# Self-attention's output projection as three f16 products from a z held in two f16 parts, with the next batch normalised one step earlier

## The chip, the cores and the metric

One core of one Trainium2 chip runs the whole program. The metric is the device time of one execution in microseconds (us). Engines are named as in the profile: PE is TensorE's matmul, PEld its weight load, DVE is VectorE, ACT is ScalarE, POOL is GpSimd, SP is SyncE.

## The reference

A decoder block over 32 batches of 128 tokens of width 128, in f32: self attention (16 heads of 64, causal), cross attention (16 heads of 8, with 128 context rows), and a mixture of 8 experts. The change touches self attention alone, and in it the last product and the normalisation of the input:

```
x = _layernorm(resid_stream, ln_w, ln_b)
...
pattern = jax.nn.softmax(scores, axis=-1)
z = jnp.einsum('bhqk,bkhe->bqhe', pattern, v)
attn_out = jnp.einsum('bqhe,hed->bqd', z, W_o) + b_o
```

## The kernel before

The program has three stages one after the other: self attention over all 32 batches, cross attention over all batches, and the experts. The last two batches of self attention are interleaved with the first steps of cross attention (`run_joined`).

Self attention is written out by hand as a pipeline over batches, and every engine runs the same function `self_attention(b, parity, valid, steps)` for b = -2 up to 32. Each batch has four steps g = 0 to 3. In one pass over b the engines work on three batches: the input of batch b+2 is normalised and transposed, the projections q, k, v of batch b+1 are made, the scores and softmax of batch b are made, and z and the output of batch b-1 are made. `valid(k)` says whether batch b+k exists. Each engine works through its own list in the order written; semaphores alone order the engines, and there are no queues or planners between them.

What the change touches, in one batch:

- Step 2, PE: z of batch b-1 as 32 entries of small f32 products into two PSUM banks, ps0 and ps1 (semaphore `sa_z_in_bank`). ACT copies each bank into the SBUF tile `zT` (L554, `sa_z_taken`).
- Step 2, DVE: the sums of unit 2 (L667, L670), then `xn`, the normalised input of batch b+2 (L720), which waits for `rstd` from POOL (`sa_rstd`, L395).
- Step 3, PE: transposes `xn` into ps7 (L979), transposes one more unit of probabilities (L1022), waits for `sa_z_taken` and for `sa_xT_taken`, and then multiplies `zT` by `wo`: eight f32 products of 128x128 that add up in another part of ps7 (L1033, shown by the profile as L971, the helper `mm`).
- Step 3, DVE: takes the transposed input out of ps7 as `xT` (L677, `sa_xT_taken`), sums unit 3, and adds the output to the residual `x_all` (L726) after `sa_output`.
- The next pass begins on PE with the scores of units 0 and 1, for which DVE's `nmax` (L660) waits.

An f32 product is one matmul in the code and two entries in the profile's counts. The projections q, k, v (`w1_hi`, `w1_lo`, `xT_hi`, `xT_lo`) are already made in three f16 products: high by high, high by low, low by high.

Of the kernel before, what the change touches and what calls it, by code (L numbers as in the profile page):

```python
# [23 lines left out]
P = 128  # L24
# [24 lines left out]
NORM_SCALE = 256.0  # L49
W_SCALE = 256.0  # L50
H_SCALE = 16.0
MASKED = -3.0e38


# [44 lines left out]
def build(nc, x, ctx, W_q, W_k, W_v, W_o, b_q, b_k, b_v, b_o, ln_w, ln_b, w_qkv, w_proj, b_proj,  # L99
          gate_w, gate_proj_w, up_proj_w, down_proj_w, out):  # L100
    es = ExitStack()
    with es:
# [27 lines left out]
        w1_hi = sb("w1_hi", [P, 3, H, E1], F16)  # L130
        w1_lo = sb("w1_lo", [P, 3, H, E1], F16)
        wo = sb("wo", [P, PAIRS, D])
        bq = sb("bq", [P, PAIRS])
        bk = sb("bk", [P, PAIRS])
        bv = sb("bv", [P, PAIRS])
# [22 lines left out]
        probs = sb("probs", [P, 4, 512])  # L158
        probsT = sb("probsT", [P, 4, 512])
        zT = sb("zT", [P, PAIRS, P])  # L160
        nmax = sb("nmax", [P, 8, 4])
        rsum = sb("rsum", [P, 8, 4])
        rinv = sb("rinv", [P, 8, 4])
# [82 lines left out]
        sa_scores = sem("sa_scores"); sa_max = sem("sa_max"); sa_exp = sem("sa_exp")  # L246
        sa_sums = sem("sa_sums"); sa_inverse_sums = sem("sa_inverse_sums")
        sa_probs = sem("sa_probs"); sa_pT_in_bank = sem("sa_pT_in_bank"); sa_pT_taken = sem("sa_pT_taken")
        sa_z_in_bank = sem("sa_z_in_bank"); sa_z_taken = sem("sa_z_taken"); sa_output = sem("sa_output")
        sa_residual = sem("sa_residual")  # L250

        ca_stats = sem("ca_stats"); ca_mean_var = sem("ca_mean_var"); ca_var_eps = sem("ca_var_eps")
# [258 lines left out]
        def _(act):  # L511
# [8 lines left out]
            for i, w in enumerate((wq, wk, wv)):  # L520
                act.wait_ge(qkv_loaded[i], 16)
                nc.scalar.activation(w1_hi[:, i, :, :], w[:, :, :], ACT.Copy, scale=W_SCALE).then_inc(w1_high_ready, 1)

            def self_attention(b, parity, valid, steps):
                def copy_transposed(g):
                    off, u, _ = back(b, parity, g, 2, G1)
                    if valid(off):
                        act.wait_ge(sa_pT_in_bank, G1 * (b + off) + u + 1)
                        nc.scalar.copy(probsT[:, u, :], ps[6][:, :]).then_inc(sa_pT_taken, 1)  # L529

                def exponentials(u):
                    if valid(0):
                        act.wait_ge(sa_max, G1 * b + u + 1)
                        for i in range(HPG):
                            last = nc.scalar.activation(probs[:, u, i * P:(i + 1) * P],  # L535
                                                        ps[u][:, i * P:(i + 1) * P], ACT.Exp,
                                                        bias=nmax[:, u, i:i + 1])
                        last.then_inc(sa_exp, 1)

                for g in steps:  # L540
                    if g == 0:
                        copy_transposed(0)
                        exponentials(0)
                        exponentials(1)
                    if g == 1:
                        copy_transposed(1)
                        exponentials(2)
                    if g == 2 and valid(-1):
                        n = b - 1
                        if valid(-2):  # L550
                            act.wait_ge(sa_output, n)
                        for half in range(HALVES):
                            act.wait_ge(sa_z_in_bank, HALVES * n + half + 1)
                            nc.scalar.copy(zT[:, 4 * half:4 * half + 4, :], ps[half][:, :]).then_inc(sa_z_taken, 1)  # L554
                    if g == 2:
                        copy_transposed(2)
                        exponentials(3)
                    if g == 3:
                        copy_transposed(3)
                    if g == 3 and valid(1):  # L560
                        n, np_ = b + 1, (parity + 1) % 2
                        for half in range(2):
                            act.wait_ge(sa_projected, 6 * n + 5 + half)
                            nc.scalar.activation(v1[:, np_, 512 * half:512 * half + 512], ps[4 + half][:, :], ACT.Copy,
                                                 scale=1.0 / (X1_SCALE * W_SCALE)).then_inc(sa_v_taken, 1)
# [85 lines left out]
        def _(dve):  # L651
# [4 lines left out]
            def self_attention(b, parity, valid, steps):  # L656
# [15 lines left out]
                for g in steps:  # L672
                    if g == 3 and valid(2):
                        dve.wait_ge(sa_xT_in_bank, b + 3)
                        if valid(1):
                            dve.wait_ge(sa_x_low, b + 2)
                        nc.vector.tensor_scalar(xT[:, :], ps[7][:, 0:P], lnwb[:, 0:1], lnwb[:, 1:2],  # L677
                                                ALU.mult, ALU.add).then_inc(sa_xT_taken, 1)

                    if g == 0:  # L680
                        maximum(0)
                        maximum(1)
                    if g == 1:
                        sums(0, 0)
                        maximum(2)
                        sums(0, 1)
                        maximum(3)
                    if g >= 2:
                        sums(0, g)

                    if valid(1) and g < 2:
                        n, np_ = b + 1, (parity + 1) % 2
                        for half in range(2):
                            dve.wait_ge(sa_projected, 6 * n + 2 * g + half + 1)
                            tiles = ps[4 + half][:, :].rearrange("p (t q) -> p t q", t=4)
                            own = slice(4 * half, 4 * half + 4)
                            if g == 0:
                                last = nc.vector.scalar_tensor_tensor(  # L698
                                    out=qT[:, np_, own, :], in0=tiles,
                                    scalar=E1 ** -0.5 / (X1_SCALE * W_SCALE), in1=bcast(bq[:, own], P),  # L700
                                    op0=ALU.mult, op1=ALU.add)
                            else:
                                last = nc.vector.scalar_tensor_tensor(
                                    out=kT[:, np_, own, :], in0=tiles, scalar=1.0 / (X1_SCALE * W_SCALE),
                                    in1=bcast(bk[:, own], P), op0=ALU.mult, op1=ALU.add)
                            last.then_inc(sa_qk_taken, 1)

                    if valid(2):
                        n = b + 2
                        if g == 0:  # L710
                            if valid(-2) and not valid(-3):
                                dve.wait_ge(x_rest_loaded, 16)
                            dve.sem_inc(alone)
                            nc.vector.bn_stats(bst[:, 0, :], x_all[:, n, :]).then_inc(sa_stats, 1)
                            dve.wait_ge(sa_stats, n + 1)
                            dve.sem_inc(alone)
                            nc.vector.bn_aggr(mv[:, 0, :], bst[:, 0, :]).then_inc(sa_mean_var, 1)
                        if g == 2:
                            dve.wait_ge(sa_rstd, n + 1)
                            nc.vector.tensor_scalar(xn[:, :], x_all[:, n, :], mv[:, 0, 0:1], rstd[:, 0:1],  # L720
                                                    ALU.subtract, ALU.mult).then_inc(sa_norm, 1)
                    if g == 3 and valid(-1):
                        n = b - 1
                        dve.wait_ge(sa_output, n + 1)
                        dve.wait_ge(sa_bias_added, n + 1)
                        nc.vector.tensor_tensor(x_all[:, n, :], ps[7][:, P:2 * P], x_all[:, n, :],  # L726
                                                ALU.add).then_inc(sa_residual, 1)

            def prepare():

# [12 lines left out]
            def prepare_cross():  # L743
# [8 lines left out]
                for dst, i, f in ((wqR, 0, E2 ** -0.5), (wkR, 1, 1.0)):  # L752
                    nc.vector.memset(dst[:, :, :, 3, :], 0.0).then_inc(quad_weights_ready, 1)
                    for t in range(4):
                        heads = wqkvT[:, i, 32 * t:32 * t + 32].rearrange("p (l e) -> p l e", e=E2)
                        nc.vector.tensor_scalar(dst[:, t, :, 0:3, :], heads.unsqueeze(2).to_broadcast([P, 4, 3, E2]),
                                                f, None, ALU.mult).then_inc(quad_weights_ready, 1)

                dve.wait_ge(bv_wo_summed, 1)
                dve.wait_ge(row_biases_loaded, 32)  # L760
# [208 lines left out]
        def _(pe):  # L969
# [3 lines left out]
            def self_attention(b, parity, valid, steps):  # L973
                for g in steps:
# [50 lines left out]
                    if g == 3 and valid(-1):  # L1025
                        n = b - 1
                        pe.wait_ge(sa_z_taken, HALVES * n + HALVES)
                        if valid(2):
                            pe.wait_ge(sa_xT_taken, b + 3)
                        if not valid(1):  # L1030
                            pe.wait_ge(ca_xT_taken, 1 if valid(0) else 2)
                        for i in range(PAIRS):
                            last = mm(ps[7][:, P:2 * P], zT[:, i, :], wo[:, i, :], i == 0, i == PAIRS - 1)  # L1033
                        last.then_inc(sa_output, 1)
                    if valid(1) and g < 3:

# [286 lines left out]
```

## Time and profile before

| what | value |
|---|---|
| runs | 1156.07, 1158.15, 1158.4 us; median 1158.15 us |
| the profiled execution's own time | 1158.08 us |
| its span, first to last instruction | 1156.2 us |
| busy: PE, PEld | 1074.3 us (93%), 800.0 us (69%) |
| busy: DVE, ACT, POOL | 830.5 us (72%), 674.7 us (58%), 457.6 us (40%) |
| mean granted TensorE clock | 0.981 of full speed |

The steady part of self attention lies between about 47 and 435 us of the span, and one batch takes 13.41 us there. Times in a row are from the span's start. A group of several instructions is printed as one row: its start, the time from there to the end of the last one, and after "x" their count. The bracket at a row's end is the idle time before it and what ended that.

### The profile page before, as it was taken

Reading aid. Unit: us, or ns where it says so; the run is one execution under the profiler, and the core shown is the slowest. Engines: PE = TensorE matmul, PEld = TensorE weight load, DVE = VectorE, ACT = ScalarE, POOL = GpSimd, SP = SyncE. Lnnn points to the kernel's source line nnn. Section 1 sums busy time; section 2 is a strip of 40 time slices with the busy share of each in tenths; the row PEclk is TensorE's granted clock in tenths of the full one; section 3 lists DMA queues with packets and bytes.
Section 4 is the critical chain, followed back from the end, with each engine's and each line's share of the span. In section 5 each row is a group of like instructions: output and inputs, shape, how many; then the busy total and the mean of one; then the engine's idle time right before and its main releaser. Section 6 shows DMA issues by size and latency. Waiting matters only on the chain.

```text
span 1156.2 us, 30982 instructions
## 1 busy us (share of the span) xinstructions
PE 1074.3 (93%) x12235; PEld 800.0 (69%) x12235; DVE 830.5 (72%) x1921; ACT 674.7 (58%) x1510; POOL 457.6 (40%) x799
## 2 busy tenths in 40 slices
PE   5999999999999998989999999999966999999997
PEld 4788888888888886667767677677643666565664
DVE  4776667776667774677777777777737788888887
ACT  2666666666656665555555565565534755555554
POOL 3444444444444444244344354453322522222222
PEclk9999999999999999899999999999976999999999
DMA  7000000000000000000000000002100000000000
GB/s 169 2 2 2 2 2 2 1 2 2 2 1 2 2 1 10 11 11 15 11 15 11 11 16 11 12 16 68 55 1 0 2 10 11 11 10 11 10 11 10
DMA packets 20658, 16.01 MB, mean 14 GB/s; under 512 B 7042, under 2 KB 18596, under 8 KB 20516
## 3 DMA queue, kind: packets, MB, share of 16 engines
q1 hardware_dynamic: 20176, 13.90, 4.6%
q8 instruction: 98, 1.61, 0.6%
q10 hardware_dynamic: 340, 0.14, 0.1%
q14 instruction: 44, 0.36, 0.1%
HBM read 11.94 MB, written 2.10 MB: 12 GB/s over the span
## 4 chain that ended last, share of the span: by engine, by line
PE 64%; issue 18%; DVE 8%; POOL 7%; ACT 2%; DMA 1%; SPq 0%; DVEq 0%; POOLq 0%
PE ps L971 56%; POOL h_lo L500 5%; PE ps L1022 5%; ACT q_shifted L572 2%; PE ps L1183 1%; DVE xT L677 1%; DMA wv<-in_L_attn_W_v 1%; DVE bst L852 1%; DVE x_all L848 1%; POOL probs L385 1%; PE ps L1213 1%; DVE padded L789 1%; DVE mv L855 1%; PE ps L1201 0%; PE ps L979 0%
## 5 line engine op out<-in xcount | busy, mean ns | idle before, releaser
L807 DVE TENSOR_REDUCE nmax<-ps 128x2 f32<-128x512 f32 x256 | 164.7, 686 | 15.4 <-PE ps L971 15.4
L597 ACT ACTIVATE probsT<-ps 128x512 f32<-128x512 f32 x256 | 139.7, 603 | 41.9 <-PE ps L971 41.0
L500 POOL TENSOR_TENSOR h_lo<-wk,h_hi 128x512 f16<-128x512 f32 x64 | 73.9, 1155 | 185.7 <-ACT h_hi L641 182.8
L535 ACT ACTIVATE probs<-ps,nmax 128x128 f32<-128x128 f32 x512 | 143.1, 384 | 6.9 <-DVE nmax L660 6.9
L529 ACT COPY probsT<-ps 128x512 f32<-128x512 f32 x128 | 75.2, 587 | 116.3 <-PE ps L1022 116.3
L385 POOL TENSOR_TENSOR probs<-probs,rinv 128x512 f32<-128x512 f32 x128 | 133.0, 1040 | 15.9 <-DVE rinv L670 15.9
L971 PE MATMUL ps<-probsT,va 128*32 128x128 f32 x2048 | 137.8, 277 | 0.0
L633 ACT ACTIVATE wq<-ps 128x512 f32<-128x512 f32 x128 | 76.6, 598 | 73.7 <-PE ps L971 73.6
L971 PEld LDWEIGHTS ps<-probsT,va 128*32 128x32 f32 x2048 | 103.0, 110 | 17.0 <-issue 6.7
L660 DVE TENSOR_REDUCE nmax<-ps 128x4 f32<-128x512 f32 x128 | 83.5, 673 | 38.9 <-PE ps L971 38.9
L955 DVE TENSOR_TENSOR h_lo<-wk,h_hi 128x512 f16<-128x512 f32 x64 | 71.8, 1122 | 43.8 <-ACT h_hi L641 43.8
L971 PE MATMUL ps<-xnT_hi,w_hi 128*128 128x512 f16 x256 | 99.7, 389 | 2.7 <-DVE wk L950 2.7
L641 ACT CAST h_hi<-wk 128x512 f16<-128x512 f32 x128 | 77.9, 618 | 40.6 <-DVE wk L950 40.5
L971 PE MATMUL ps<-xnT_lo,w_hi 128*128 128x512 f16 x256 | 99.2, 387 | 0.0
L971 PE MATMUL ps<-xnT_hi,w_lo 128*128 128x512 f16 x256 | 99.0, 387 | 0.0
L971 PE MATMUL ps<-xT_hi,w_hi 128*128 128x128 f16 x512 | 91.2, 222 | 6.2 <-DVE raw_gu L698 4.2
L971 PE MATMUL ps<-xT_lo,w_hi 128*128 128x128 f16 x512 | 91.3, 222 | 0.0
L971 PE MATMUL ps<-xT_hi,w_lo 128*128 128x128 f16 x512 | 91.3, 222 | 0.0
L971 PE MATMUL ps<-w_hi,h_hi 128*128 128x128 f16 x512 | 88.9, 219 | 2.6 <-DVE h_lo L955 2.6
L971 PE MATMUL ps<-w_hi,h_lo 128*128 128x128 f16 x512 | 89.0, 219 | 0.0
L971 PE MATMUL ps<-w_lo,h_hi 128*128 128x128 f16 x512 | 88.9, 219 | 0.0
L667 DVE TENSOR_REDUCE rsum<-probs 128x4 f32<-128x512 f32 x128 | 85.9, 671 | 3.7 <-ACT probs L535 3.7
(204 smaller groups left out, 2552.3 us busy)
## 6 DMA issues: line engine op xcount, KB each, us to landing
ctx_row<-in_ctx SPq DMA_DIRECT2D x32, 128.0 KB, 2.0
out_x<-x_all SPq DMA_DIRECT2D x8, 256.0 KB, 2.3
kT<-in_L_ffn_down_proj_w SPq DMA_DIRECT2D x1, 1024.0 KB, 10.8
wq<-in_L_attn_W_q SPq DMA_DIRECT2D x1, 512.0 KB, 5.0
wk<-in_L_attn_W_k SPq DMA_DIRECT2D x1, 512.0 KB, 8.8
wv<-in_L_attn_W_v SPq DMA_DIRECT2D x1, 512.0 KB, 10.4
wo<-in_L_attn_W_o SPq DMA_DIRECT2D x2, 256.0 KB, 6.7
x_all<-in_x SPq DMA_DIRECT2D x1, 256.0 KB, 3.0
```

Of the source, the lines that this page charges most:

```text
L385: nc.gpsimd.tensor_tensor(pr, pr, bcast(rinv[:, u, :], P), ALU.mult).then_inc(sa_probs, 1)
L500: nc.gpsimd.tensor_tensor(h_lo[:, e % 2, 0, :], hT[:, 0, :], h_hi[:, e % 2, 0, :], ALU.subtract).then_inc(hidden_low_first, 1)
L529: nc.scalar.copy(probsT[:, u, :], ps[6][:, :]).then_inc(sa_pT_taken, 1)
L535: last = nc.scalar.activation(probs[:, u, i * P:(i + 1) * P], ps[u][:, i * P:(i + 1) * P], ACT.Exp, bias=nmax[:, u, i:i + 1])
L597: last = nc.scalar.activation(probsT[:, 2 * (t % 2) + a, :], ps[2 + a][:, :], ACT.Exp)
L633: nc.scalar.activation(silu[:, i, :], ps[i][:, :], ACT.Silu, scale=1.0 / (NORM_SCALE * W_SCALE)).then_inc(silu_ready, 1)
L641: nc.scalar.copy(h_hi[:, e % 2, i, :], hT[:, i, :]).then_inc(hidden_high, 1)
L660: nc.vector.reduce_max(nmax[:, u, :], ps[u][:, :].rearrange("p (h k) -> p h k", h=HPG), AX_X, negate=True).then_inc(sa_max, 1)
L667: nc.vector.reduce_sum(rsum[:, u, :], probs[:, u, :].rearrange("p (h k) -> p h k", h=HPG), AX_X).then_inc(sa_sums, 1)
L807: last = nc.vector.reduce_max(nmax2[:, b % 2, t:t + 2, l + a], ps[a][:, :].rearrange("p (t k) -> p t k", t=2), AX_X, negate=True)
L955: nc.vector.tensor_tensor(h_lo[:, e % 2, 1, :], hT[:, 1, :], h_hi[:, e % 2, 1, :], ALU.subtract).then_inc(hidden_low_second, 1)
L971: return nc.tensor.matmul(o, l, r, start=start, stop=stop, **kw)
```

## The change

z is no longer copied as f32. ACT writes four times z as f16 (`zT_hi`), DVE writes what is left over of four times z as f16 (`zT_lo`), and both lie in the memory of the old tile `zT`. The weight `wo` is split once, at the start, into `wo_hi` and `wo_lo` (times 256). The output is 24 f16 products in place of eight f32 ones, and the residual addition divides by the scales. On DVE `xn` moves from step 2 to the end of step 1.

```diff
+            act.wait_ge(wo_loaded, 32)
+            nc.scalar.activation(wo_hi[:, :, :], wo[:, :, :], ACT.Copy, scale=W_SCALE).then_inc(wo_high_ready, 1)
...
                         for half in range(HALVES):
                             act.wait_ge(sa_z_in_bank, HALVES * n + half + 1)
-                            nc.scalar.copy(zT[:, 4 * half:4 * half + 4, :], ps[half][:, :]).then_inc(sa_z_taken, 1)
+                            nc.scalar.activation(zT_hi[:, 4 * half:4 * half + 4, :], ps[half][:, :], ACT.Copy,
+                                                 scale=Z_SCALE).then_inc(sa_z_high, 1)
...
                     if g >= 2:
                         sums(0, g)
+                    if g == 2 and valid(-1):
+                        for half in range(HALVES):
+                            dve.wait_ge(sa_z_high, HALVES * (b - 1) + half + 1)
+                            nc.vector.scalar_tensor_tensor(
+                                out=zT_lo[:, 4 * half:4 * half + 4, :], in0=ps[half][:, :].rearrange("p (t q) -> p t q", t=4),
+                                scalar=Z_SCALE, in1=zT_hi[:, 4 * half:4 * half + 4, :], op0=ALU.mult,
+                                op1=ALU.subtract).then_inc(sa_z_taken, 1)
...
-                        if g == 2:
+                        if g == 1:
                             dve.wait_ge(sa_rstd, n + 1)
                             nc.vector.tensor_scalar(xn[:, :], x_all[:, n, :], mv[:, 0, 0:1], rstd[:, 0:1],
                                                     ALU.subtract, ALU.mult).then_inc(sa_norm, 1)
...
-                        nc.vector.tensor_tensor(x_all[:, n, :], ps[7][:, P:2 * P], x_all[:, n, :],
-                                                ALU.add).then_inc(sa_residual, 1)
+                        nc.vector.scalar_tensor_tensor(out=x_all[:, n, :], in0=ps[7][:, P:2 * P],
+                                                       scalar=1.0 / (Z_SCALE * W_SCALE), in1=x_all[:, n, :],
+                                                       op0=ALU.mult, op1=ALU.add).then_inc(sa_residual, 1)
...
+                dve.wait_ge(wo_high_ready, 1)
+                nc.vector.scalar_tensor_tensor(out=wo_lo[:, :, :], in0=wo[:, :, :], scalar=W_SCALE, in1=wo_hi[:, :, :],
+                                               op0=ALU.mult, op1=ALU.subtract).then_inc(wo_low_ready, 1)
...
                         pe.wait_ge(sa_z_taken, HALVES * n + HALVES)
+                        if n == 0:
+                            pe.wait_ge(wo_low_ready, 1)
...
                         for i in range(PAIRS):
-                            last = mm(ps[7][:, P:2 * P], zT[:, i, :], wo[:, i, :], i == 0, i == PAIRS - 1)
+                            for k, (z, w) in enumerate(((zT_hi, wo_hi), (zT_hi, wo_lo), (zT_lo, wo_hi))):
+                                last = mm(ps[7][:, P:2 * P], z[:, i, :], w[:, i, :], i == 0 and k == 0,
+                                          i == PAIRS - 1 and k == 2)
```

On DVE, in every steady batch, the list before reads as follows from the end of step 1 (`kT`) to the residual of step 3. The names are those of the kernel, and the bracket names the semaphores waited for.

```order
L703 SCALAR_TENSOR_TENSOR kT<-ps,bk 128x512 [waits sa_projected] x2
L667 TENSOR_REDUCE rsum<-probs 128x4 [waits sa_exp]
L670 RECIPROCAL rinv<-rsum 128x4 [waits sa_sums]
L720 TENSOR_SCALAR xn<-x_all,mv,rstd 128x128 [waits sa_rstd]
L677 TENSOR_SCALAR xT<-ps,lnwb 128x128 [waits sa_x_low,sa_xT_in_bank]
```

The same place in the changed kernel, whose lines are numbered differently (L719 is the old L703, L736 the old L720, L686 the old L677):

```order
L719 SCALAR_TENSOR_TENSOR kT<-ps,bk 128x512 [waits sa_projected] x2
L736 TENSOR_SCALAR xn<-x_all,mv,rstd 128x128 [waits sa_rstd]
L676 TENSOR_REDUCE rsum<-probs 128x4 [waits sa_exp]
L679 RECIPROCAL rinv<-rsum 128x4 [waits sa_sums]
L702 SCALAR_TENSOR_TENSOR zT<-ps,zT 128x512 [waits sa_z_high] x2
L686 TENSOR_SCALAR xT<-ps,lnwb 128x128 [waits sa_x_low,sa_xT_in_bank]
```

`xn` now stands ahead of the sums of unit 2, and the two new instructions for `zT_lo` stand between those sums and `xT`. On PE, in step 3 and at the head of the next pass, the list before is:

```order
L979 MATMUL ps<-ident,xn 128x128 [waits sa_residual,sa_norm]
L1022 MATMUL ps<-ident,probs 128x128 [waits sa_pT_taken,sa_probs]
L1022 MATMUL ps<-ident,probs 128x128 x3
L971 MATMUL ps<-wo,zT 128x128 [waits sa_xT_taken,sa_z_taken]
L971 MATMUL ps<-wo,zT 128x128 x7
L971 MATMUL ps<-causal,ident_b 128x512 [waits sa_exp,sa_qk_taken]
```

In the changed kernel the eight `wo` products of that list are 24, in this pattern; `zT` is `zT_hi` in the first two of each three and `zT_lo` in the third:

```order
L1000 MATMUL ps<-ident,xn 128x128 [waits sa_residual,sa_norm]
L1043 MATMUL ps<-ident,probs 128x128 [waits sa_pT_taken,sa_probs]
L1043 MATMUL ps<-ident,probs 128x128 x3
L992 MATMUL ps<-wo_hi,zT 128x128 [waits sa_xT_taken,sa_z_taken]
L992 MATMUL ps<-wo_lo,zT 128x128
L992 MATMUL ps<-wo_hi,zT 128x128 x2
...
L992 MATMUL ps<-causal,ident_b 128x512 [waits sa_exp,sa_qk_taken]
```

Nothing else moved on PE, and the waits are the same two, but `sa_z_taken` is now signalled by DVE, not by ACT.

## Rows read from the trace of the kernel before

**Rows 1.** The page: busy time by engine, and granted clock in 40 slices.

```profile
PE 1074.3 (93%) x12235; PEld 800.0 (69%) x12235; DVE 830.5 (72%) x1921; ACT 674.7 (58%) x1510; POOL 457.6 (40%) x799
...
PEclk9999999999999999899999999999976999999999
```

**Rows 2.** One batch's window (length, busy by engine, clock), and PE's idle time until xT (us, times).

```profile
288.68:302.09 13.41, 13.25 (x157) 10.97 (x156) 9.34 (x21) 8.67 (x25) 5.91 (x9) 1.00 0.00 1
...
  DVE xT L677: 4.6, 29
```

**Rows 3.** The chain of waits in one batch: start, length, what.

```profile
302.32 0.42 DVE xT L677
...
302.88 3.55 PE ps L971 x34
```

**Rows 4.** Timeline of PE and PEld around the output product, and a first f16 product.

```profile
289.44 1.86 PEld L971 LDWEIGHTS ps<-wo,zT 128*128 128x128 f32 x16 [0.37 <-issue]
289.47 2.02 PE L971 MATMUL ps<-wo,zT 128*128 128x128 f32 x16 [0.16 <-DVE xT L677]
...
291.33 0.60 PE L971 MATMUL ps<-causal,ident_b 128*128 128x512 bf16 x2
...
292.95 0.66 PE L1022 MATMUL ps<-ident,probs 128*128 128x128 f32 x4
...
293.33 0.10 PEld L971 LDWEIGHTS ps<-xT_hi,w_hi 128*128 128x128 f16 x1
...
293.44 0.22 PE L971 MATMUL ps<-xT_hi,w_hi 128*128 128x128 f16 x1
```

**Rows 5.** Timeline of PE in the experts: the first of 24 products, and what follows them.

```profile
902.54 0.22 PE L971 MATMUL ps<-w_hi,h_hi 128*128 128x128 f16 x1
...
903.88 0.38 PE L971 MATMUL ps<-xnT_hi,w_hi 128*128 128x512 f16 x1
```

**Rows 6.** Timeline of DVE in one batch, end of step 1 to step 3.

```profile
298.86 1.28 DVE L703 SCALAR_TENSOR_TENSOR kT<-ps,bk 128x512 f32<-128x512 f32 x2
300.05 0.68 DVE L667 TENSOR_REDUCE rsum<-probs 128x4 f32<-128x512 f32 x1
300.76 0.18 DVE L670 RECIPROCAL rinv<-rsum 128x4 f32<-128x4 f32 x1
300.86 0.32 DVE L720 TENSOR_SCALAR xn<-x_all,mv,rstd 128x128 f32<-128x128 f32 x1
302.32 0.41 DVE L677 TENSOR_SCALAR xT<-ps,lnwb 128x128 f32<-128x128 f32 x1 [1.14 <-PE ps L979]
```

**Rows 7.** Timeline of ACT and POOL near it.

```profile
290.27 1.04 POOL L385 TENSOR_TENSOR probs<-probs,rinv 128x512 f32<-128x512 f32 x1
...
300.34 0.58 ACT L554 COPY zT<-ps 128x512 f32<-128x512 f32 x1 [0.23 <-PE ps L971]
```

**Rows 8.** DVE's groups by shape: busy us, mean ns, idle before.

```profile
L955 DVE TENSOR_TENSOR h_lo<-wk,h_hi 128x512 f16<-128x512 f32 x64 | 71.8, 1122 | 43.8 <-ACT h_hi L641 43.8
...
L776 DVE SCALAR_TENSOR_TENSOR q_part<-q_hi,low_q,ps 128x512 f16<-128x512 f16 x32 | 23.6, 737 | 1.4 <-ACT q_hi L585 1.4
...
L739 DVE SCALAR_TENSOR_TENSOR w_lo<-wq,w_hi 128x1024 f16<-128x1024 f32 x1 | 1.2, 1226 | 0.0
```

**Rows 9.** Timeline of DVE before the first scores.

```profile
25.72 0.17 DVE L761 TENSOR_SCALAR gateT<-ps 128x8 f32<-128x8 f32 x1 [0.26 <-PE ps L971]
...
27.36 1.29 DVE L660 TENSOR_REDUCE nmax<-ps 128x4 f32<-128x512 f32 x2 [0.87 <-PE ps L971]
```

**Rows 10.** Timeline where self attention joins cross attention (b = 31, 32).

```profile
446.39 1.21 ACT L554 COPY zT<-ps 128x512 f32<-128x512 f32 x2
...
447.00 0.72 DVE L776 SCALAR_TENSOR_TENSOR q_part<-q_hi,low_q,ps 128x512 f16<-128x512 f16 x1
...
447.77 1.16 PE L971 MATMUL ps<-xT,wkR 128*128 128x128 f32 x8 [0.61 <-DVE q_part L776]
...
456.58 2.05 PE L971 MATMUL ps<-wo,zT 128*128 128x128 f32 x16 [0.68 <-ACT zT L554]
```

More of the change, by code:

```diff
@@ L51 @@
 H_SCALE = 16.0
+Z_SCALE = 4.0
 MASKED = -3.0e38
@@ L132, in build @@
         wo = sb("wo", [P, PAIRS, D])
+        wo_hi = sb("wo_hi", [P, PAIRS, D], F16)
+        wo_lo = sb("wo_lo", [P, PAIRS, D], F16)
         bq = sb("bq", [P, PAIRS])
@@ L160, in build @@
         zT = sb("zT", [P, PAIRS, P])
+        zT_halves = zT[:, :, :].rearrange("p t q -> p (t q)").bitcast(F16).rearrange("p (a t q) -> p a t q", a=2, t=PAIRS)
+        zT_hi, zT_lo = zT_halves[:, 0, :, :], zT_halves[:, 1, :, :]
         nmax = sb("nmax", [P, 8, 4])
@@ L248, in build @@
         sa_probs = sem("sa_probs"); sa_pT_in_bank = sem("sa_pT_in_bank"); sa_pT_taken = sem("sa_pT_taken")
-        sa_z_in_bank = sem("sa_z_in_bank"); sa_z_taken = sem("sa_z_taken"); sa_output = sem("sa_output")
+        sa_z_in_bank = sem("sa_z_in_bank"); sa_z_high = sem("sa_z_high"); sa_z_taken = sem("sa_z_taken"); wo_high_ready = sem("wo_high_ready"); wo_low_ready = sem("wo_low_ready"); sa_output = sem("sa_output")
         sa_residual = sem("sa_residual")
```

## The prediction

> **What bounds the kernel now.** First the page: PE is busy 93% of the span, and the granted clock is 0.9 or more of full speed in all the slices of self attention, the first 16 [rows 1]. Then the window of one batch: 13.41 us long with PE busy 13.25, DVE 9.34, ACT 8.67, POOL 5.91, at clock 1.00, the 2.4 GHz level [rows 2]. So PE bounds the batch, and what it does not fill is small. Then the chain of waits in that batch, to see whether PE is alone: the chain leaves PE at one place only, for DVE's xT, which starts at 302.32 and lets PE go on at 302.88 with the output product [rows 3]. The reader is to see that an instruction of PE saved behind that point shortens the batch, and that an instruction of DVE added ahead of xT lengthens it once DVE's own slack is used up. PE waits for xT in 29 batches [rows 2]; those are the steady ones.
>
> **Step 1, the product itself.** After the wait the weight load of the f32 product starts at 289.44 and the next work, the causal mask, starts at 291.33: 1.89 us for the eight products [rows 4]. The f16 price is in this kernel already: 24 products of the same shape, three parts for each piece, added up in one PSUM region, run in the experts from 902.54 to 903.88, which is 1.34 us or 56 ns each [rows 5]. After a gap an f16 load starts 0.11 ahead of its product (293.33, 293.44) [rows 4]. So the new stretch is 0.11 + 1.34 = 1.45 us, and PE saves 1.89 - 1.45 = **0.44 us** a batch. The other bound: reckoned from product to product it is 291.33 - 289.47 = 1.86 against 1.34, 0.52. I take 0.44, since the wait in front exposes the first load here.
>
> **Step 2, the work added on DVE.** Two instructions of 128x512, PSUM and f16 in, f16 out, stand between the sums of unit 2 and xT. The trace has no such form. Nearest are the kT pair: same instruction, one operand in PSUM, an immediate scalar; two of them end 1.28 after their start and the next instruction starts at 300.05, 1.19 after it, so each occupies **0.60** although it is 0.68 long [rows 6]. The f16 output costs nothing there: 1024 elements out of SBUF in this very form take 1.226 us, no more than twice 0.61 [rows 8]. The form with f16 in and out and PSUM is 0.737 long, about 0.06 more, but it has a per-partition scalar where the new one has an immediate [rows 8]; by it each would occupy 0.66. I take 0.60, for the immediate.
>
> **Step 3, what covers it.** DVE has xn started at 300.86 and xT at 302.32, 1.46 apart with 1.14 idle between them, waiting for PE's transpose of xn [rows 6]. xn itself occupies 0.32 less the overlap of 0.08 that the kT pair shows, 0.24. The free stretch is 1.46 - 0.24 = 1.22 us. xn moves ahead of the sums, which shifts them by 0.24 and leaves the total as it was. The new pair needs 2 x 0.60 = 1.20. So xT can start 0.02 before PE's transpose lets it: the cover just suffices, and I put the lateness at **0**. With 0.66 each it is 1.32 - 1.22 = 0.10 late, and with 0.74 each, end to end, 0.26. Without the move of xn the transpose would have waited for the pair; with it, xn is ready at about 300.4 and PE asks for it about 302.
>
> The pair's own wait, for ACT's second half, is not felt: ACT ends it at 300.92 [rows 7], and DVE comes to the second at 300.29 + 0.71 + 0.10 + 0.60 = 301.70 (the sums 0.24 later than 300.05, the spacing of the sums and the reciprocal as in [rows 6]). Behind the pair wait xT and the sums of unit 3, nothing else. The scale and the f16 output on ACT stand in the place of a copy of the same size and I put them at nothing; their cover is the 0.78 between 300.92 and 301.70.
>
> **Step 4, does the gain survive the round?** After the output product PE goes to the scores, for which DVE has been waiting; both move up together. The first later wait that is not PE's own is for the probabilities of unit 2: POOL's multiplication starts at 290.27 and takes 1.04, so it ends at 291.31 [rows 7], while PE asks for them after the mask and the scores, at 292.95 [rows 4]. With PE 0.44 earlier 1.2 us are left. So the steady batches give 29 x 0.44 = **12.8 us**.
>
> **Step 5, the ends.** At the start ACT splits wo once and DVE once; DVE's part takes what one of the same shape takes, 1.23, and occupies 1.15 [rows 8]. DVE there has 0.26 idle before gateT and 0.87 before the first nmax, 1.13 in all [rows 9]: nothing, or 0.02. Where b = 30 there is no xT to wait for and PE saves its 0.44. Where b = 31, DVE's q_part of cross attention now stands behind the pair: ACT ends the two z halves at 446.39 + 1.21 = 447.60, the second zT_lo takes 447.64 to 448.32, q_part starts at 448.26, not at 447.00, and PE has been waiting for it [rows 10]. That costs 1.26, less the 0.44 of the product: +0.82. Where b = 32 nothing covers the last zT_lo. The f32 product starts there at 456.58, released by ACT, and ends at 458.63 [rows 10]; now zT_lo takes that start and 0.68, to 457.26, with 0.04 to PE, and then 0.11 + 23 x 0.056 + 0.22 for the 24 products gives 458.92: +0.29. The ends sum to -0.44 + 0.82 + 0.29 = +0.7.
>
> **Sum.** -12.8 + 0.7 = -12.1. The profiled execution took 1158.08 us for its span of 1156.2, and the median of the runs is 1158.15, the same within 0.1. 1158.1 - 12.1 = **1146.0 us**.
>
> **The rivals.**
>
> *A, DVE becomes the bound by a little (17%).* Speaking for it: the cover in step 3 is 0.02 us, that is, none. If the two instructions occupy their full 0.68, xT is 0.14 late; at 0.74, 0.26 late. The gain is then 0.30 to 0.18 a batch, 8.7 to 5.2 in all, and the time 1158.1 - 8.7 + 0.7 = 1150.1 to 1153.6. Against it: the kT pair overlaps. The Trainium skill, "VectorE: DVE Perf Modes", section "The DRAIN you can't avoid", says that the next operation does not start until the pipe is empty. By that rule each would occupy its whole length; here the rows after the kT pair, starting 0.09 before its end, speak against so much [rows 6].
>
> *B, slower (6%).* The new instruction runs like L955, the subtraction of an f16 part from an f32 one with f16 out: 1.122 long [rows 8], 1.04 occupied. Then xT is 2.08 - 1.22 = 0.86 late, the batch longer by 0.86 - 0.44 = 0.42, and the time 1158.1 + 12.2 + 0.7 = 1171. It decides from (1.22 + 0.44) / 2 = 0.83 occupied each. Against it: L955 reads both operands from SBUF, but so does L739, at 1.226 for twice the elements [rows 8], so that the slowness is not of the form alone; the new one reads one from PSUM, as kT does. The Trainium skill, "SBUF — State Buffer", section "Terms", says that VectorE and GpSimd hold a shared port pair exclusively and that the loser blocks.
>
> *C, the f16 products don't run at 56 ns (3%).* The loads are 0.10 long [rows 4]; if each stood in front of its product, 24 would take 2.4 us and the batch would be 0.6 longer, 1158.1 + 18 = 1176. It decides from 1.78 / 24 = 74 ns. The experts' rows speak against it [rows 5].
>
> *D, the gain is swallowed by another wait (4%).* Time 1158 to 1159, with the 0.7 of the ends. Step 4 leaves 1.2 us at the nearest.
>
> **How the numbers follow.** The forecast has 70%. Its own range is 1143 (0.52 a batch, 30 batches, +0.7) to 1149.0 (0.34 a batch: 0.10 late). To leave out no more than 2 in 10 the range takes in A: 1143 to 1153.6. B, C and D, 13%, are left out. A difference under 0.2% (2.3 us) can't be told from no change here. Faster by more: the forecast and A, and a little is taken off for what joins them, 0.88. Within it: D, 0.05. Slower: B and C, 0.07.
>
> **What the profile would show.** Right: the batch is 12.97 long; the 24 products fill about 1.4 us between xT's release and the mask; DVE's idle time before xT is gone or under 0.1; PE's transpose of xn waits for nothing. Step 2 is wrong if the pair takes over 1.3 us; step 1 if the stretch after the wait is not 1.45; step 4 if PE has a new wait elsewhere in the batch. The forecast is wrong, above all, if the pair starts late or lasts longer, because nothing is left between it and xT.

## The result, and the profile after

| | before | changed |
|---|---|---|
| median of the runs | 1158.2 us (1156.07 to 1158.4, 4 runs) | 1142.51 us (1141.44 to 1143.47, 4 runs) |
| ratio, 95% interval | | 0.9868 (0.9851 to 0.9886) |
| run again later | 1157.94 us (9 runs) | 1143.12 us (4 runs), 0.9879 (0.9865 to 0.9893) |
| profiled execution: time, span | 1158.08, 1156.2 us | 1141.44, 1139.7 us |

The change is faster by 15.7 us, where 12.1 was forecast; the median lies 0.5 us below the stated range, and the repeat 0.1 above its lower end. The way was right, the size was not. The kernel before ran again beside every later run, with medians of 1157.6 to 1157.9 us; every ratio below is to those.

The page of the changed kernel, busy time by engine and the granted clock in 40 slices, to be held against [rows 1]:

```profile
PE 1052.5 (92%) x12458; PEld 782.9 (69%) x12491; DVE 868.7 (76%) x1986; ACT 676.6 (59%) x1511; POOL 457.5 (40%) x799
...
PEclk9999999999999999999999999999977999999999
```

DVE is up by 38 us, the 64 new instructions less what overlaps, and PE is down by 22. Some 3 of these 22 are not real: this trace lacks 33 of PE's 12491 product records, and in the repeat, which has all of them, PE is at 1055.8 us. The timeline of DVE over one steady batch shows where that work went, where [rows 6] had 1.14 us of idle time:

```profile
282.69 1.29 DVE L669 TENSOR_REDUCE nmax<-ps 128x4 f32<-128x512 f32 x2 [1.24 <-PE ps L992]
...
288.48 1.28 DVE L719 SCALAR_TENSOR_TENSOR kT<-ps,bk 128x512 f32<-128x512 f32 x2
289.67 0.34 DVE L736 TENSOR_SCALAR xn<-x_all,mv,rstd 128x128 f32<-128x128 f32 x1
289.93 0.68 DVE L676 TENSOR_REDUCE rsum<-probs 128x4 f32<-128x512 f32 x1
290.64 0.18 DVE L679 RECIPROCAL rinv<-rsum 128x4 f32<-128x4 f32 x1
290.74 1.26 DVE L702 SCALAR_TENSOR_TENSOR zT<-ps,zT 128x512 f16<-128x512 f32 x2
291.94 0.41 DVE L686 TENSOR_SCALAR xT<-ps,lnwb 128x128 f32<-128x128 f32 x1
...
295.57 1.29 DVE L669 TENSOR_REDUCE nmax<-ps 128x4 f32<-128x512 f32 x2 [1.24 <-PE ps L992]
```

Two things are to be seen. The pair takes 290.74 to xT at 291.94, 1.20 us, and no idle time is printed ahead of xT any more. And the batch, from one nmax to the next, is 295.57 - 282.69 = 12.88 us. Over 27 steady batches the mean is 12.886, 0.52 shorter than the 13.407 of the kernel before.

The timeline of PE and PEld in the same batch, for [rows 4]:

```profile
291.63 0.27 PE L1000 MATMUL ps<-ident,xn 128*128 128x128 f32 x1
...
292.47 0.10 PEld L992 LDWEIGHTS ps<-wo_hi,zT 128*128 128x128 f16 x1 [0.37 <-issue]
292.50 0.22 PE L992 MATMUL ps<-wo_hi,zT 128*128 128x128 f16 x1 [0.16 <-DVE xT L686]
```

The record of the first product of the causal mask, which follows the 24, is missing in this batch. The repeat of the same kernel has it:

```profile
292.64 0.22 PE L992 MATMUL ps<-wo_hi,zT 128*128 128x128 f16 x1 [0.16 <-DVE xT L686]
...
293.98 0.59 PE L992 MATMUL ps<-causal,ident_b 128*128 128x512 bf16 x2
```

So the 24 products take 1.34 us, 56 ns each. And in the kernel before, the transpose of xn stands here:

```profile
302.01 0.27 PE L979 MATMUL ps<-ident,xn 128*128 128x128 f32 x1
```

PE's transpose of xn waits for nothing in the changed kernel either, and xT starts 0.31 behind it, as before (302.01 and 302.32). The first load stands 0.03 ahead of its product, and the product starts 0.56 behind the start of xT (291.94, 292.50). With f32 it was 302.32 and 302.88, 0.56 too [rows 3]. The f16 load costs nothing extra at this place.

The chain of waits of the changed kernel has moved, though no wait has grown (start, length, what):

```profile
290.01 0.61 DVE rsum L676
...
290.74 1.26 DVE zT L702 x2
291.99 0.37 DVE xT L686
292.37 0.14 issue
292.50 1.50 PE ps L992 x24
```

(The 1.50 reaches to the end of the last product and not to the start of the next work, which is why it is more than 1.34.) It runs through DVE from nmax to xT, since both engines arrive there within 0.05 us of each other (the run with a third instruction, below). That the chain changes its engine says that they are level, not that one of them has become slower.

### The profile page after: what moved, and what is told of

Same layout as the page of the kernel before. It is cut to its first block, busy times and chain, and to the rows that moved or that the text cites. A ratio compares the mean times of both kernels' runs of the same rounds, so it can differ in the third digit from the quotient of the medians.

```text
span 1139.7 us, 31527 instructions
## 1 busy us (share of the span) xinstructions
PE 1052.5 (92%) x12458; PEld 782.9 (69%) x12491; DVE 868.7 (76%) x1986; ACT 676.6 (59%) x1511; POOL 457.5 (40%) x799
## 3 DMA queue, kind: packets, MB, share of 16 engines
q1 hardware_dynamic: 20176, 13.90, 4.6%
## 4 chain that ended last, share of the span: by engine, by line
PE 41%; DVE 29%; issue 19%; POOL 6%; ACT 3%; DMA 1%; DVEq 0%; SPq 0%; POOLq 0%
PE ps L992 37%; DVE nmax L669 6%; POOL h_lo L505 6%; DVE rsum L676 5%; DVE zT L702 3%; DVE kT L719 3%; DVE raw_gu L714 2%; ACT q_shifted L581 2%; PE ps L1208 1%; DVE rinv L679 1%; DVE xT L686 1%; DMA wv<-in_L_attn_W_v 1%; DVE bst L873 1%; DVE x_all L869 1%; DVE bst L730 1%
## 5 line engine op out<-in xcount | busy, mean ns | idle before, releaser
L828 DVE TENSOR_REDUCE nmax<-ps 128x2 f32<-128x512 f32 x256 | 164.6, 685 | 15.9 <-PE ps L992 15.7
```

What stands on the lines that cost most here:

```text
L828: last = nc.vector.reduce_max(nmax2[:, b % 2, t:t + 2, l + a], ps[a][:, :].rearrange("p (t k) -> p t k", t=2), AX_X, negate=True)
```

## The experiments

A batch is read each time as the distance of two neighbouring starts of the nmax pair in the steady part. It repeats within 0.01 us but for one batch in all the traces (13.80, in the run with a third instruction), where whole runs of one kernel differ by 2 us and more, and in that run by 8.

**The products without the work on DVE.** The pair is taken out, and the third product of each three takes `zT_hi`:

```diff
-                        for half in range(HALVES):
-                            dve.wait_ge(sa_z_high, HALVES * (b - 1) + half + 1)
-                            nc.vector.scalar_tensor_tensor(
...
-                                                 scale=Z_SCALE).then_inc(sa_z_high, 1)
+                                                 scale=Z_SCALE).then_inc(sa_z_taken, 1)
...
-                            for k, (z, w) in enumerate(((zT_hi, wo_hi), (zT_hi, wo_lo), (zT_lo, wo_hi))):
+                            for k, (z, w) in enumerate(((zT_hi, wo_hi), (zT_hi, wo_lo), (zT_hi, wo_hi))):
```

> Leaves out the low part of z: ACT's f16 copy releases the product directly, DVE has no zT_lo instructions, and the third product of each three takes zT_hi again, so that PE has the same 24 f16 products. Theory T (each f16 product costs PE 56 ns and its first load is hidden as the f32 one was, so that the product saves 0.52 us a batch; DVE's pair is just covered): the batch is 12.89 long as in the changed kernel, and the two places at the end where the pair is not covered (0.67 and 0.21) come back, so about 0.9 under the changed kernel's 1142.5: 1141.6. DVE idles some 1.2 before xT. Rival R1 (the product saves 0.44 as forecast and 0.08 came from somewhere on DVE's side): the batch is 12.97 or longer, 1144 or more. Rival R2 (DVE's pair already sets the changed kernel's batch): the batch is shorter than 12.89, by the lateness of the pair.

Measured: 1139.82 us (4 runs), 0.985 (0.9836 to 0.9865). DVE's timeline:

```profile
282.28 1.29 DVE L669 TENSOR_REDUCE nmax<-ps 128x4 f32<-128x512 f32 x2 [1.24 <-PE ps L985]
...
289.27 0.34 DVE L729 TENSOR_SCALAR xn<-x_all,mv,rstd 128x128 f32<-128x128 f32 x1
...
291.54 0.41 DVE L686 TENSOR_SCALAR xT<-ps,lnwb 128x128 f32<-128x128 f32 x1 [1.13 <-PE ps L993]
...
295.17 1.29 DVE L669 TENSOR_REDUCE nmax<-ps 128x4 f32<-128x512 f32 x2 [1.24 <-PE ps L985]
```

The batch is 12.89 with 1.13 us of idle time ahead of xT. So the 0.52 is the products' alone (R1 falls), and the pair costs a steady batch nothing (R2 falls). The whole time fell by 2.7 against the changed kernel, not by 0.9. The trace shows 1.85 of it: I had taken the ends' losses net of the products' gain there. The last two passes take 12.41 and 6.69 us without the pair and 13.54 and 7.41 with it, so the pair costs 1.13 + 0.72 = 1.85 there. The other 0.9 lies within the scatter of whole runs.

**The work on DVE without the products.** The kernel before, with:

```diff
+                    if g == 2 and valid(-1):
+                        for half in range(HALVES):
+                            dve.wait_ge(sa_z_high, HALVES * (b - 1) + half + 1)
+                            nc.vector.scalar_tensor_tensor(
+                                out=z_rest[:, 4 * half:4 * half + 4, :], in0=ps[half][:, :].rearrange("p (t q) -> p t q", t=4),
+                                scalar=2.0, in1=zT[:, 4 * half:4 * half + 4, :], op0=ALU.mult,
+                                op1=ALU.subtract).then_inc(sa_z_taken, 1)
...
-                        if g == 2:
+                        if g == 1:
```

> The kernel before with its eight f32 products and f32 zT, plus DVE's part alone: two instructions of the form of the zT_lo pair stand between the sums of unit 2 and xT (they read ps0, ps1 and the f32 zT and write a tile that nobody reads), they release the output product, and xn is in step 1. Theory T (the pair is just covered): the batch stays 13.41, the start gains about 0.4, the join of the stages loses 0.67 and 0.21, so +0.4 on the kernel before: 1158.6. Rival (the pair shows on the path): each 0.1 of lateness adds 2.9; by whole lengths of 0.68 the time would be 1162.

Measured: 1158.22 us (10 runs), 1.0014 (1.0003 to 1.0024); the batch is 292.29 - 278.88 = 13.41. The pair is hidden beside f32 products too (here it reads zT in f32, and is 1.26 us long as with f16). It shows in the last two passes, 13.96 and 7.93 us in place of 12.85 and 7.21. The profiled execution was the longest of the ten, 1163.3 us, but its steady batches are no longer for that.

**xn moved alone, and everything but the move.** The one line `if g == 2:` ahead of xn, in the kernel before turned to 1, in the changed kernel turned back to 2.

> The kernel before with xn moved to step 1 and nothing else. Theory T: steady batches stay 13.41, since PE asks for xn long after either place; in the pipeline's batch 0, where PE did wait for xn, 0.39 is saved once: 1157.8 where the kernel before has 1158.2, which the clock on the wall can't tell and the trace can. Rival (the move itself gives part of the 0.52 a batch): the batch is shorter than 13.41, and 0.08 a batch would be 1155.8.

> The changed kernel with xn back in step 2, behind the zT_lo pair. Theory T: DVE reaches xn at about 1.20 + 0.6 after the end of kT and the sums, ends it some 0.4 after PE asks for it, PE's transpose of xn waits, and xT with all behind it is 0.4 to 0.5 later: a batch of 13.3 to 13.4 in place of 12.89, 29 times 0.45 is 13, time 1154 to 1157. Rival: the move was not needed, because xT waits for DVE anyway: the batch stays within 0.1 of 12.89, 1143 to 1145.

Measured for the move alone: 1156.26 us (10 runs), 0.9988 (0.9979 to 0.9998). The batch is 278.94 - 265.54 = 13.40: the steady part does not change. The pipeline's batch 0 takes 10.00 us (27.02 to 37.02) in place of 10.38 (27.36 to 37.74), 0.38 where 0.39 was expected once. The rest of the 1.3 us between the medians can't be placed: in the profiled executions the later stages take 697.4 and 697.5 us.

Measured with xn back in step 2: 1157.5 us (10 runs), 0.9998 (0.9988 to 1.0008). The gain is gone. DVE's timeline:

```profile
285.90 1.26 DVE L702 SCALAR_TENSOR_TENSOR zT<-ps,zT 128x512 f16<-128x512 f32 x2
287.08 0.34 DVE L736 TENSOR_SCALAR xn<-x_all,mv,rstd 128x128 f32<-128x128 f32 x1
287.84 0.41 DVE L686 TENSOR_SCALAR xT<-ps,lnwb 128x128 f32<-128x128 f32 x1 [0.42 <-PE ps L1000]
...
291.47 1.29 DVE L669 TENSOR_REDUCE nmax<-ps 128x4 f32<-128x512 f32 x2 [1.24 <-PE ps L992]
```

Now xn stands right in front of xT with PE's transpose between them, 0.42 us in which DVE can only wait, and the batch is 291.47 - 278.11 = 13.36, in the mean 13.355. The move gives nothing in a steady batch alone, and 0.47 us beside the pair. The 0.05 a batch that are left don't show in the whole time; pass 31 took 15.16 us here, in place of the changed kernel's 13.54, at a lower clock (last section).

**How much slack is left on DVE.** A third instruction of the pair's form:

```diff
-                        for half in range(HALVES):
+                        for k, half in enumerate((0, 0, 1)):
...
+                                out=h_lo[:, 0, 0, :].rearrange("p (t q) -> p t q", t=4) if k == 0 else zT_lo[:, 4 * half:4 * half + 4, :],
```

> The changed kernel with a third DVE instruction of the form of the zT_lo pair in front of it in every batch (it writes a tile that is free then). Theory T (0.02 of slack is left on DVE before xT): the batch is longer by 0.60 - 0.02 = 0.58, 13.47, and the time 1142.5 + 29 x 0.58 + 1.2 for the end = 1160.5. Rival (DVE had more slack than the trace shows, for the transpose of xn sets xT): longer by 0.4 or less, under 1155.

Measured: 1160.79 us (7 runs), 1.003 (1.0011 to 1.0048); the batch is 293.41 - 279.97 = 13.44, 0.55 longer.

```profile
288.01 0.66 DVE L702 SCALAR_TENSOR_TENSOR h_lo<-ps,zT 128x512 f16<-128x512 f32 x1
288.59 1.28 DVE L702 SCALAR_TENSOR_TENSOR zT<-ps,zT 128x512 f16<-128x512 f32 x2
289.79 0.40 DVE L686 TENSOR_SCALAR xT<-ps,lnwb 128x128 f32<-128x128 f32 x1
```

The three occupy 1.78 us, 0.58 to 0.60 each, and one of them costs 0.55: the slack is 0.02 to 0.05 us, and with one instruction more the change is a small loss.

**A third of the products.** The list of three pairs is cut to `((zT_hi, wo_hi),)`.

> Leaves out two of the three products (high by low and low by high), so 8 f16 products stand for 24; all else is the changed kernel. Theory T (56 ns a product with nothing fixed beside it, and all behind xT moves up): the batch is shorter by 16 x 0.0556 = 0.89, 12.00; over 32 batches that is 28.5 less: 1114. Rival (a fixed cost of the stretch, a first load, or another wait that is reached early, such as POOL's probabilities, of which about 0.2 is left): the batch is over 12.05, the time above 1116.

Measured: 1116.95 us (2 runs), 0.9646 (0.9627 to 0.9666); the batch is 288.49 - 276.49 = 12.00, in the mean 11.99, 0.90 shorter for 16 products, 56 ns each. The eight that are left take 0.44 us, 55 ns each, so nothing fixed stands beside them:

```profile
286.31 0.61 PE L992 MATMUL ps<-wo_hi,zT 128*128 128x128 f16 x8 [0.16 <-DVE xT L686]
286.75 0.59 PE L992 MATMUL ps<-causal,ident_b 128*128 128x512 bf16 x2
```

The whole is 3 us over the forecast. The span behind the last residual is 698.7 us here and 696.2 in the changed kernel, and that stage is the same code; and pass 31 took 13.90 us, where 13.54 less 0.89 would be 12.65, because the clock fell there too (last section).

**What still stops PE in a batch.** PE gives the next batch's first scores ahead of the output product, and DVE adds the output later:

```diff
+def early(b):
+    return 1 <= b < NB - 3
...
+                        if early(b):
+                            scores(b + 1, (parity + 1) % 2, 0)
                         if valid(2):
                             pe.wait_ge(sa_xT_taken, b + 3)
...
                         maximum(1)
+                        if early(b - 1):
+                            add_output(b - 2)
```

> The changed kernel with another order on PE: in batches 1 to 28 of the pipeline the scores of units 0 and 1 of the next batch come ahead of the output product, after a wait for zT_lo alone, and DVE adds the output to the residual after the first two maxima of the next batch. Theory T (what is left of PE's idle time in a batch is the wait for xT, some 0.32 between the last transpose and the first output product, and DVE has time once its maxima start earlier): PE has no wait left, the batch is 12.89 - 0.32 = 12.57, and 28 of them save 9.0: 1142.5 - 9.0 = 1133.5. Rival (DVE's list sets the batch by itself, whatever PE does): the batch stays 12.89 and the time 1142. Other rival: PE comes too early for POOL's probabilities of unit 2 and waits there: between the two.

Measured: 1132.98 us (4 runs), 0.9785 (0.977 to 0.9799). The chain of waits over one batch:

```profile
271.79 0.11 PE ps L1028
271.90 0.44 PE ps L1054 x4
272.33 2.97 PE ps L1001 x42
275.30 0.45 PE ps L1054 x4
275.75 2.86 PE ps L1001 x42
278.61 0.59 PE ps L1054 x4
279.20 3.24 PE ps L1001 x56
282.43 0.59 PE ps L1054 x4
283.02 1.29 PE ps L1001 x6
284.31 0.11 PE ps L1028
```

It never leaves PE. The batch is 286.43 - 273.90 = 12.53 us, 0.36 shorter. So the changed kernel had that much of PE's time left in the wait for xT, and DVE's list does not set the batch by itself. (In its trace PE stands idle for 0.32 us there; which part of the new order gives the other 0.04 is not shown.)

**The join of the stages.** For b = 31 the pair goes behind q_part:

```diff
-                    if g == 2 and valid(-1):
+                    if g == (3 if b == NB - 1 else 2) and valid(-1):
                         for half in range(HALVES):
```

First tried together with the scores first:

> As the run with the scores first, and where self attention joins cross attention (b = 31) the zT_lo pair stands in step 3, behind q_part of cross attention, not ahead of it. Theory T: q_part is no longer late by the pair, which the trace of the kernel without the pair put at 1.13 there, and the output product of that batch is not reached before the pair is done: 1.1 less than the run with the scores first, 1132.4. Rival (the pair then delays the output product in its turn): no gain, 1133.5.

Measured: 1134.03 us (4 runs), 0.9788 (0.9774 to 0.9803), no less than without this step, though the pass itself fell from 15.16 us (411.88 to 427.04) to 12.41 (411.16 to 423.57). The later stages took 699.9 us in this profile and 698.4 in the one with the scores first alone. The step alone, the changed kernel and both steps were then run beside each other:

> The changed kernel with one step of DVE moved: where self attention joins cross attention (b = 31) the zT_lo pair stands in step 3, behind q_part, not ahead of it. Theory T (the pair stood in front of q_part, PE waited 2.0 us for it): from the residual of batch 30's pass to that of the next 12.41 in place of 13.54 in the profiled run of the changed kernel, with PE's wait under 1 us, so 1.1 less where the clock does not fall in that wait and up to 2.7 less where it does (the runs with a third instruction, with xn in step 2 and with the scores first had the clock at 1.2 GHz behind that wait and took 15.2 to 15.8 there). Against the changed kernel run again beside it: 1.1 to 2.7 less, about 1140.5. Rival: the start of cross attention begins at a lower clock and takes the gain back (20 us at mean clock 0.61 in the run that had this step and the scores first, 0.83 in the changed kernel): a difference under 1.

> The changed kernel once more, unchanged, as the measure for the others of this call. Theory T: self attention as before, a batch of 12.89 and 15.2 less than the kernel before up to the last residual, give or take the clock at the join; what is left of the total difference comes from the granted clock at the start of cross attention: 1142 to 1143.5. Rival (the change also saves something in the later stages by itself): their span is again 1.3 under that of the kernel before, at whatever clock.

> The kernel with the scores first and the moved pair at the join, once more and with more rounds: a batch of 12.53, the join 12.41; 28 x 0.36 = 10.1 under the run with the moved pair alone, 1131 to 1134. Rival: the time differs from it by less than 8, because the later stages take it back.

Measured: the step alone 1140.76 us (4 runs), 0.9854 (0.984 to 0.9867); the changed kernel 1143.12 (4 runs); both steps 1131.07 (5 runs), 0.9772 (0.9759 to 0.9786). By the medians the step is worth 2.4 us; the trace shows 1.1 of it, pass 31 at 12.40 (421.50 to 433.90) in place of 13.52, and the rest can't be placed. The kernel with both steps ran 3.0 us faster here than in its first run, so the medians of two runs don't settle a step of this size. The scores first give 9.7 more by the medians and 9.9 by the traces, from the first nmax to the last residual. The last is the fastest kernel here that makes all three products, 2.3% under the kernel before and 1.1% under the changed one. With the pair moved, PE's wait for q_part falls from 2.0 us to 0.6. In the repeat of the changed kernel, and with the step alone:

```profile
433.23 1.16 PE L992 MATMUL ps<-xT,wkR 128*128 128x128 f32 x8 [1.99 <-DVE q_part L797]
```

```profile
430.66 1.16 PE L994 MATMUL ps<-xT,wkR 128*128 128x128 f32 x8 [0.61 <-DVE q_part L799]
```

## Why the prediction was right in its way and wrong in its size

The trace gives the gain at marks along the program, before against changed:

| mark | before | changed | gained so far |
|---|---|---|---|
| nmax of batch 0 | 27.36 | 27.27 | 0.09 |
| nmax of batch 1 | 37.74 | 37.26 | 0.48 |
| residual in pass 30 | 438.61 | 422.57 | 16.04 |
| residual in pass 31 | 451.46 | 436.11 | 15.35 |
| last residual | 458.67 | 443.52 | 15.15 |
| end of the span | 1156.2 | 1139.7 | 16.5 |

- **Step 1 failed, by its size.** It chose 0.44 us a batch "since the wait in front exposes the first load here", and put 0.52 as the other bound. The runs show the other bound: 15.56 us over 30 passes is 0.519 each, the kernel without the pair has it too, and 16 products less save 0.90 with nothing fixed. The row behind the 0.11 was a load made while PE was still at other products, not one after this wait. Behind this wait the load stands 0.03 ahead of its product in either type (289.44 and 289.47 in [rows 4], 292.47 and 292.50 above), and 0.11 - 0.03 is the whole 0.08 that was missed. The term should have been 13.2 + 2.4 = 15.6 for the 29 batches and b = 30.
- **Step 2 was right.** 0.60 occupied for each of the pair: 1.20 from its start to xT, and 1.18 where xn follows it, which no transpose holds back (285.90 to 287.08); each is 0.678 long in the median. The 0.66 and 0.74 did not come.
- **Step 3 was right, and as tight as it said.** Lateness 0, forecast slack 0.02, and a third instruction costs 0.55 of its 0.6. The move of xn is what makes it so: without it the batch is 13.36.
- **Step 4 was right.** No new wait of PE appears in a batch, even with 0.90 taken out behind xT.
- **Step 5 was nearly right at the end and wrong at the start.** Forecast +0.82 and +0.29 in the last two passes, measured +0.69 and +0.20. Against the kernel without the pair, the pair costs 1.13 in the first of them where 1.26 was forecast, and the product saves the 0.44; in the second the pair costs 0.72 as forecast, and the product saves 0.52, so that the 0.09 there is Step 1's error again. It missed that in batch 0, where there is no output product and no pair, PE did wait for xn; the move saves 0.39 there (0.38 in the run of the move alone). wo_lo is hidden, as said.
- **The later stages** gained 1.35 us in the profiled executions, forecast 0. That isn't shown to be the change's: in its repeat the last residual is 697.2 us before the end, in the kernel before 697.5, and the same stages vary more than that between the profiles (last section).

The errors add up: 2.36 + 0.48 + 0.13 + 0.09 + 1.35 = 4.4, which is 16.5 - 12.1. Of these, the 1.35 and the 0.09 ahead of the first nmax, which lies between 25.8 and 27.4 us in the traces here, are scatter. Without them the change is worth 15.06 us, and 1158.1 - 15.06 = 1143.0 lies between its two medians. That is 3.0 over the forecast's 12.1: Step 1 with 2.4 (0.08 for each of 30 passes), the start with 0.4, and the last two passes with 0.2. That the first median fell out of the range and the repeat into it is chance.

The low end of the range was off too. It took 0.52 for 30 batches and then the +0.7 of the ends, in which b = 30 is contained already: counted once, 29 x 0.52 and ends of -0.52 + 0.74 + 0.21 give 1143.4, with nothing for the start. The bound that turned out to be the true value stood at the very edge.

Of the rivals, A, taken as whole lengths of 0.68, would have made xT 0.14 late; the pair occupies 1.20 and not 1.36, so A fell. The Trainium skill, "VectorE: DVE Perf Modes", section "The DRAIN you can't avoid", says that the next operation does not start until the pipe is empty, and adds that one that is not held starts earlier. Read as whole lengths the first half does not agree with the trace; with the second half the rows agree, for xT starts at 291.94 and the pair ends at 292.00. B fell: the subtraction with one operand in PSUM runs at 0.68, not 1.12. Why L955 is slow was not tried. C fell with 56 ns a product, D with the steady gain of 0.52.

## What to carry to other kernels

When an engine stops at one wait in each round, sum the other engine's list up to that point and compare: work that fits the idle time in front of the wait is free to the last hundredth, and what exceeds it is paid nearly in full, so the order there (here one instruction moved by a step) can decide the whole gain. Read the cost of a first instruction after a wait from a row after that same wait, measured to the release, not from a first instruction elsewhere; if the type is another, the row of the old type there is still the nearer one. And after such a change ask what the two engines now wait for together: independent work placed in front of the wait (here the next scores) gave another 0.36 us a batch.

## What was not expected of the hardware

The same wait has two prices. In pass 31, PE's 2.0 us wait for q_part left the granted clock at its full level in both profiles of the changed kernel and in the one with the work on DVE alone. In four other runs it fell to half, 1.2 GHz, within 1 us behind that wait: with the scores first (the pass took 15.16 us in place of 13.54), with xn in step 2 (15.16) and with a third of the products (13.90, where 12.65 was to be had), all with 2.0 us of waiting too, and with a third instruction (15.77, with 2.6 us of waiting). With the scores first the eight products behind the wait take 1.87 us, where the repeat of the changed kernel, above, has 1.16 behind a wait of the same length:

```profile
422.43 1.87 PE L1001 MATMUL ps<-xT,wkR 128*128 128x128 f32 x8 [1.99 <-DVE q_part L806]
```

Windows of 2 us with the scores first (length, busy by engine, clock, DMA):

```profile
422.00:424.00 2.00, 1.57 (x8) 1.57 (x9) 1.24 (x3) 0.40 (x2) 2.00 (x5) 0.67 0.00 0
424.00:426.00 2.00, 2.00 (x16) 1.94 (x15) 0.00 (x0) 1.27 (x2) 1.24 (x3) 0.50 0.03 8
```

What decides it at a wait of the same length is open. And the first 20 us behind the last residual run at a mean clock that differs from profile to profile, with the same code. The span from the last residual to the end goes with it in part:

| mean clock of the 20 us | profiles | last residual to the end |
|---|---|---|
| 0.83 | changed kernel, xn in step 2, third instruction, both steps again | 696.2, 695.9, 696.2, 696.4 us |
| 0.74 | kernel before, changed kernel again, join alone | 697.5, 697.2, 697.1 us |
| 0.66 | xn moved alone, products alone, scores first, work on DVE alone | 697.4, 696.8, 698.4, 701.9 us |
| 0.61, 0.57 | both steps in their first run, a third of the products | 699.9, 698.7 us |

The same clock stands beside 696.8 and 701.9, so it isn't the whole cause, and what else differs is open. In windows of the changed kernel and of its repeat:

```profile
443.80:463.80 20.00, 15.81 (x157) 11.38 (x159) 14.16 (x28) 7.89 (x15) 6.08 (x15) 0.83 0.03 8
```

```profile
444.00:464.00 20.00, 16.18 (x153) 11.46 (x155) 13.91 (x27) 7.63 (x15) 6.08 (x15) 0.74 0.03 8
```

So single microseconds of a whole run's time say little here, while the length of a batch in the steady part repeats to 0.01 in all but one batch.
